# Head sums and gate logits as matmuls of 128 columns in an attention, FFN and expert layer kernel

## The reference, cut to what matters

```python
q, k = sigmoid(heads(Wq, bq)), sigmoid(heads(Wk, bk)); v = heads(Wv, bv)
sink_in   = normal / einsum('bhld,bhld->bhl', q + EPS, cumsum(k) + EPS)
src_out   = normal / einsum('bhld,bhld->bhl', k + EPS, cumsum(q) + EPS)
cons_sink = einsum('bhld,bhld->bhl', q + EPS, cumsum(k * src_out) + EPS) / normal
cons_src  = einsum('bhld,bhld->bhl', k + EPS, cumsum(q * sink_in) + EPS) / normal
sink_alloc = sigmoid(cons_sink); e = exp(clip(cons_src, -1, 1))
src_comp = e / cumsum(e) * normal
kv = cumsum(k x (v * src_comp)); x = (q * sink_in / normal) . kv * sink_alloc
h = layernorm(inputs + x @ Wo + bo); y = layernorm(h + gelu(h @ W1 + b1) @ W2 + b2)
# expert layer, on x2 = layernorm(inputs + y)
logits = x2 @ gate_w.T + gate_b; scores = softmax(logits); top_v, top_i = top_k(scores, 2)
# for each chosen expert: relu(x2 @ wi.T + bi + (x2 @ A_e.T) @ B_e.T) @ wo.T + bo, times top_v.sum()
out = layernorm(x2 + expert sum)
```

## Time and profile before

| | |
|---|---|
| median of 3 runs | 442.75 us (441.65 to 443.66) |
| the profiled execution | 443.3 us, of which 441.5 us are the span of its instructions |
| PE, PEld, DVE, ACT, POOL busy | 89%, 63%, 76%, 47%, 51% of the span |
| mean granted TensorE clock | 0.924 |
| matmul instructions of the head sums (L349), of the logits (L444) | 256, 64 |

### The profile page before, as it was taken

How to read it: one execution, slowest core, us unless ns; L and a number is a source line. 1 busy time by engine, 2 the same in 40 slices (tenths; PEclk the granted TensorE clock), 3 DMA queues, 4 the chain that set the end, 5 groups by cost and what they waited for, 6 DMA issues and landing times.

```text
span 441.5 us, 6398 instructions
## 1 busy us (share of the span) xinstructions
PE 391.1 (89%) x2080; PEld 279.4 (63%) x2080; DVE 334.5 (76%) x795; ACT 207.4 (47%) x375; POOL 224.6 (51%) x263
## 2 busy tenths in 40 slices
PE   8996869488999899899989999999998999889992
PEld 3555766276656767487738775677658775865651
DVE  3549955497779896998789888979799779843532
ACT  2230215334556176437654575537662673275541
POOL 2016224783259435853578329923894368644211
PEclk9888857886999989999899999989999999999997
DMA  8226005400072003700180008200640035000000
GB/s 269 83 59 157 1 1 127 110 2 1 0 172 68 1 0 85 178 1 1 31 221 12 1 2 204 59 0 3 152 111 1 1 84 131 1 1 26 0 25 24
DMA packets 19858, 26.58 MB, mean 60 GB/s; under 512 B 1649, under 2 KB 9969, under 8 KB 19825
## 3 DMA queue, kind: packets, MB, share of 16 engines
q1 hardware_dynamic: 19680, 25.96, 22.8%
q10 hardware_dynamic: 144, 0.21, 0.2%
HBM read 7.29 MB, written 2.10 MB: 21 GB/s over the span
## 4 chain that ended last, share of the span: by engine, by line
PE 42%; DVE 25%; issue 14%; POOL 13%; DMA 3%; ACT 2%; POOLq 0%; DVEq 0%; SPq 0%; ACTq 0%
POOL prod L811 8%; PE pB L349 5%; DVE kv L1005 5%; PE pY L430 5%; PE pG L420 5%; DVE cum_kv L1011 4%; PE pY L508 4%; DMA vb<-vs 3%; PE pG L497 3%; PE pG L490 2%; PE pO L403 2%; DVE cum_ks L901 2%; PE pG L484 2%; DVE cum_q L901 2%; PE pA L337 2%
## 5 line engine op out<-in xcount | busy, mean ns | idle before, releaser
L811 POOL TENSOR_TENSOR prod<-cum_kv,q_fac 128x512 f32<-128x512 f32 x64 | 94.0, 1474 | 34.7 <-DVE cum_kv L1011 28.3
L403 PEld LDWEIGHTS pO<-s_wor,prod 128*128 128x128 f32 x512 | 67.4, 205 | 29.6 <-POOL prod L811 21.5
L403 PE MATMUL pO<-s_wor,prod 128*128 128x128 f32 x512 | 72.5, 294 | 14.1 <-POOL prod L811 13.9
L1005 DVE TENSOR_TENSOR kv<-k,vb 128x512 f32<-128x512 f32 x64 | 53.5, 838 | 7.8 <-DMA vb<-vs 7.8
L798 POOL TENSOR_TENSOR var_eps<-mv,s_con 128x4 f32<-128x4 f32 x32 | 10.0, 312 | 78.6 <-DVE mv L1025 78.6
L1011 DVE TENSOR_TENSOR_SCAN cum_kv<-p_ones,cum_kv,kv 128x512 f32<-128x512 f32 x32 | 40.5, 1275 | 0.6
L1011 DVE TENSOR_TENSOR_SCAN cum_kv<-p_ones,kv 128x512 f32<-128x512 f32 x32 | 38.5, 1214 | 0.5
L508 PEld LDWEIGHTS pY<-s_moe,gel 128*128 128x128 f32 x256 | 33.5, 204 | 6.6 <-issue 4.8
L508 PE MATMUL pY<-s_moe,gel 128*128 128x128 f32 x256 | 34.9, 289 | 0.0
L724 ACT ACTIVATE relu<-pG,s_att 128x512 f32<-128x512 f32 x28 | 19.2, 685 | 33.2 <-PE pG L490 33.1
L430 PEld LDWEIGHTS pY<-s_ffn,gel 128*128 128x128 f32 x256 | 31.0, 193 | 4.4 <-issue 4.4
(11 more groups left out here) (160 smaller groups left out, 795.8 us busy)
## 6 DMA issues: line engine op xcount, KB each, us to landing
vb<-vs SPq DMA_DIRECT2D x64, 256.0 KB, 4.6
xT<-x_t SPq DMA_DIRECT2D x8, 256.0 KB, 4.8
xt<-x SPq DMA_DIRECT2D x8, 256.0 KB, 5.1
out<-y SPq DMA_DIRECT2D x8, 256.0 KB, 2.3
s_moe<-moe_w SPq DMA_DIRECT2D x1, 836.0 KB, 10.4
s_wor<-wo_rep SPq DMA_DIRECT2D x1, 512.0 KB, 8.2
s_ffn<-ffn_w SPq DMA_DIRECT2D x1, 512.0 KB, 8.8
s_con<-consts SPq DMA_DIRECT2D x1, 502.0 KB, 4.7
```

What stands on the lines that cost most here:

```text
L403: mm = pe.matmul(pO3[:, s, :], prod[:, m % 4, s * P:(s + 1) * P], s_wor[:, m, :], start=False, stop=(m == DH - 1), skip_group_check=True)
L811: pool.tensor_tensor(prod[:, m % 4, :], cum_kv[t.par][:, m, :], q_fac[t.par][:, :], ALU.mult).then_inc(prod_ready, 1)
L1005: dve.tensor_tensor(kv[:, m % 3, :], k[t.par][:, :], vb[:, m, :], ALU.mult).then_inc(kv_ready, 1)
```

## The change

The same matmuls stream 128 columns. Instead of the 16 columns of `headsum`, the 128 columns of `s_att` that end with `headsum` are streamed (112 columns of `wv` come before it), and instead of the 8 of `gate` the 128 of `s_moe` that end with `gate` (120 columns of the LoRA matrix before it). The wanted columns are the last of each result. The pieces are computed from the last to the first, so that each one's 112 or 120 columns of padding fall on columns that a later piece overwrites, or that nobody reads. The places of `p_den`, `p_cons`, `p_cume` in pB and of `p_log` in pM move accordingly. The number of instructions, their waits and their order among the other work stay.

```diff
+SUMS_AT, CONS_AT, LOG_AT = P - HEADS, 2 * P + 6 * HEADS, P - EXPERTS
...
-        p_den, p_cons, p_cume = pB[:, 0:2 * HW], pB[:, 2 * HW:4 * HW], pB[:, 4 * HW:5 * HW]
-        p_log = pM[:, 0:SUB * EXPERTS].rearrange("p (s e) -> p s e", s=SUB)
+        p_den, p_cons, p_cume = pB[:, SUMS_AT:SUMS_AT + 2 * HW], pB[:, CONS_AT:CONS_AT + 2 * HW], pB[:, 0:HW]
+        p_log = pM[:, LOG_AT:LOG_AT + SUB * EXPERTS].rearrange("p (s e) -> p s e", s=SUB)
...
-                dst = (p_den, p_cons)[pair]
+                base = (SUMS_AT, CONS_AT)[pair]
+                wide_sum = s_att[:, W_ATT["headsum"][1] - P:W_ATT["headsum"][1]]
...
-                for s in range(SUB):
-                    mm = pe.matmul(dst[:, at + s * HEADS:at + (s + 1) * HEADS], src[:, s * P:(s + 1) * P], att("headsum"),
-                                   start=True, stop=True)
+                for s in reversed(range(SUB)):
+                    end = base + at + (s + 1) * HEADS
+                    mm = pe.matmul(pB[:, end - P:end], src[:, s * P:(s + 1) * P], wide_sum, start=True, stop=True)
...
-                for s in range(SUB):
-                    mm = pe.matmul(p_log[:, s, :], x2T[t.par][:, s * P:(s + 1) * P], moe("gate"), start=True, stop=True)
+                wide_gate = s_moe[:, W_MOE["gate"][1] - P:W_MOE["gate"][1]]
+                for s in reversed(range(SUB)):
+                    mm = pe.matmul(pM[:, s * EXPERTS:s * EXPERTS + P], x2T[t.par][:, s * P:(s + 1) * P], wide_gate,
+                                   start=True, stop=True)
```

## The result

The changed kernel takes 430.64 us in the median (429.72 to 432.17, 6 runs) against 441.58 us before (440.05 to 443.66, 6 runs beside them): ratio 0.9755, 95% interval 0.972 to 0.979, 10.9 us less. The forecast was 433.5 us, 9.3 less. The profiled executions lie a little further apart, 430.02 and 443.3 us. The kernel before varies more from run to run than the changed one (3.6 against 2.5 us here), and so does its mean clock, which lies mostly between 0.924 and 0.943, against 0.964 to 0.973. Four disturbed runs among the later ones (1982.2, 497.5, 444.7 and 444.5 us) are in none of the ratios.

A forecast was written before the change was run, and what follows sets the result against it. PE was taken as the bound, busy 391 us (89%), partly at a lowered clock. Opening 2.4 + third step 1.4 + full steps 5.8 - later results 0.3 = 9.3 us less: 433.5 us, range 429.5 to 441.0.

The forecast's parts named there:

- Clock as the lever: Around the head sums: a gap together with 16-column streams lowers PE's clock; wider streams keep it, mean 0.95 or more.
- The rival of falls from gaps alone: Whole kernel: PE's gaps alone cause the falls, so all stay; 443.0 us, chance 0.09.
- Pace of the padded matmuls: All 320 padded instructions: weight loads set the pace, so padding costs 0, at most 1.3 us, at either clock.
- the 2 us by the Trainium skill's figure: Low-clock stretches: some 110 ns more for each of some 20 padded instructions, 2 us; the forecast decided against it.
- Later results: Readers of padded groups: last piece at most 97 ns later, three waits on the path, 0.3 us; bounds 0 and 2.3.
- the slower rival: All 24 DVE waits for padded groups: no fall goes and each 97 ns delay counts; 445.0 us, chance 0.05.
- Opening: Tile 0's opening: both low-clock stretches behind head sums go, 2.4 us less; bounds 1.0 and 2.7.
- Tile 1's step: Low stretch 53.8 to 70.8 us: clock may return for a part, 0 to 3 us; taken as 0.
- Third step: Fall at 101.6 us goes, so the qk group and project_v get shorter: 1.4 us less; bounds 1.0 and 1.5.
- Full steps: Five steps of the full pipeline: four lose their fall and match the one at clock 1.00, 5.8 us; bounds 3.6 and 6.8.
- What is late next: Full step at full clock: PE's list with the wait for xT holds it at 45.9 us; no new bound below.
- The case between, some falls stay: Two of four full-step falls left, one in the third step back, opening as forecast: 437.4 us, chance 0.16.

The follow-up runs named there:

- 16-column kernel with fillers: Kernel before, head sums of 16 columns, with useless 512-column matmuls in PE's gaps at each pair from tile 1's second step on: 0.9888, 435.57 us.
- places and order alone: Changed kernel with the new bank places and reversed order kept, but 16 and 8 columns streamed as before: ratio 0.9977 to the kernel before.
- second profile of the change: The changed kernel itself, unaltered, measured once more against the kernel before: 431.45 against 439.23 us, ratio 0.9802.
- logits alone: Changed kernel with only the gate logits streaming 128 columns, head sums 16: ratio 1.0003 to the kernel before.
- both pairs: Changed kernel with both pairs of head sums streaming 128 columns, gate logits 8 as before: ratio 0.9811 to the kernel before.

## Why the prediction was right, by its steps

**Clock as the lever.** Right, and shown by the 16-column kernel with fillers, against the run with places and order alone. The falls behind head sums went in the opening, the third step and the full steps, as forecast; the one that begins in the second pair of tile 1 stands behind idle times and stayed. The rival of falls from gaps alone fell: the gap ahead of the first pair is still 0.94 us in the profile after, with the clock at 1.00. That a fall stood behind a wait of 2.0 us in one run, and four in the idle early steps, leaves its other half true: idle time counts, and the streams around it count too. Narrow pairs have no fall behind them in every step, and what decides between one step and the next is open.

**Pace of the padded matmuls, 0.** Right: 0.89 us for eight, before and after. The 115 ns of L403, which I had as an upper bound, are not its pace either: 22 of the 23 distances in that group are 111 to 113 ns, and the one behind its first instruction, where the stream comes from the 8-column logits, is 192. A padded group behind an idle time has the same (184 ns behind its first instruction): 0.97 us for the first eight, 0.08 more than 16 columns took in the same place. It is hidden in the idle time around it. At the lower clock my 229 ns had a short wait in them; from one instruction to the next 16 columns take 213 to 215 ns, and so do 128 (212 to 215 in the second profile of the change, in the group from 54.69 us, past its first instruction). These rows rule out the 2 us by the Trainium skill's figure (TensorE: Matmul & The Clock Gate, LDWEIGHTS) for that case.

**Later results, 0.3 us.** The delay is there, the cost is not. In every full step DVE's reciprocal of the sums now waits 0.12 us for PE, where it waited 0.03. So the sentence that DVE had other work until the sums were there was true by a hair. The 0.1 us is taken up by DVE's next wait, for PE's transposes, 1.38 us where it was 1.47, and undisturbed full steps take 46.0 us with 16 and with 128 columns. The long waits in the list fell from 6.7 to 4.8 us, but the clock has a part in them too. The bound of 2.3 us, and with it the slower rival, was far from the mark.

**Opening, 2.4 us.** 2.8 in the profiles, of which 0.55 come from an earlier start of the first head sums (10.00 against 10.55 us), so 2.2 for what I had summed.

**Tile 1's step, 0 with up to 3.** 1.6 us. The clock came back for a part of 53.8 to 70.8, the stretch from 40 us was half as long (3.4 against 6.8 us), and PE's share of the path was more than none. The 0 was a choice within the bounds.

**Third step, 1.4 us.** 3.0 us in the profiles. This is the term that was mis-sized. I had priced the two groups behind the first head sums, and had expected another fall in the idle time after them, so that the rest of 101.6 to 111.8 would stay low. It did not come: after has no low stretch between 86.5 us and the end of the full steps. Where it did come, with the fillers in the kernel of 16 columns, the step took 1.4 us less than before (53.8 against 55.2), which is the price that I had given.

**Full steps, 5.8 us.** 6.0. The step at 1.00 was the right measure for the others.

**What is late next.** Half wrong. I said PE's list with its wait for xT holds a full step at the full clock. Neither 1.4 to 1.7 us more work for PE in its gaps nor the wait for xT taken away moved it. PE holds it only in its two parts of the chain, 20 of 45.8 us, and DVE holds nearly all of the rest. My reason, that PE is busy for 43 to 45 us of a step, doesn't make it the bound. A fall shows in full where it lands in PE's parts, and elsewhere less what PE has to spare there.

**Sum.** 9.3 us forecast, 10.9 measured in the first comparison, 7.8 in the later one (439.23 less 431.45): the difference between the two is as large as the forecast's error, and lies mostly in the kernel before. The profiles' 13.4 us are of two executions, one of them among the kernel's slowest. The means of three profiles with narrow pairs (before, places alone, logits alone) less those of three with both padded (the change twice, both pairs) are a better measure of the terms: opening 2.1, tile 1's step 1.2, third step 2.4, full steps 5.1, together 10.7 us. By them the forecast was low by 1.2 and 1.0 in the steps of tiles 1 and 2, and high by 0.3 and 0.7 in the opening and the full steps.

**The case between, some falls stay.** Not met with both pairs padded. Falls stayed with one pair padded, and there the time doesn't go by their number: four stay in the full steps either way, and the first pair alone gives nothing to be seen (0.9982), the second about half of the gain (0.9875).

## What to carry to other kernels

Where every short matmul brings a weight load of its own, look whether more streamed columns are free, as they were here up to 128. Narrow streams with gaps between them were followed, some 2 us later at most, by half the clock in work that has nothing to do with them. Look in the clock's windows for what stands ahead of each fall, and fill all such places of a loop or none: with one left, the fall came there. A kept clock is worth what lies on the path. Behind the second pair, where PE holds the chain, a fall cost all of the 1.7 us that PE lost; in the early steps, where PE is often idle, 20 us of it were worth some 1.4. And filling PE's waits changes nothing where another engine holds the chain.

## What the runs showed of the hardware

- Eight matmul instructions with a weight load each take 0.89 us at the full clock with 16, 32, 64 or 128 columns of 32-bit floats, 111 to 113 ns each. At the lower clock it is 213 to 215 ns each with 16 columns (kernel before, from 55.54 us) and 212 to 215 with 128 (second profile of the change, from 54.69 us): the pace goes with the granted clock.
- Behind an idle time of PE eight such instructions take 0.89 us with 16 columns and 0.97 with 128.
- Falls of the clock stood 0.3 to 2.2 us behind the start of a pair's second narrow group, with a gap of 0.4 to 0.95 us at the pair, in three or four of five full steps. With 64 or 128 columns the same gaps (0.94 us ahead of the first pair) had no fall behind them, and with 16 columns and the gaps filled there was none in the full steps either. One fall stood behind a wait of 2.0 us among wide streams; waits of 1.6 and 1.8 us had none.
